# Four-layer block kernel on one core: pair products in four banks, decays between two gate products, and a reordered last-but-one block

## The reference

```python
# third layer, with h the state of 128 channels x 16
x_ssm, z = split(layernorm(x) @ W_in)
x_ssm = silu(causal_conv(x_ssm))          # 4 taps
dt = softplus(x_ssm @ dt_w + dt_b)
Bm, Cm = x_ssm @ B_w, x_ssm @ C_w
h = exp(min(dt * A, 0)) * h + (dt * x_ssm) * Bm      # step by step over time
y = h . Cm + x_ssm * D_param
out = residual + (y * silu(z)) @ W_out
# fourth layer, w1, w2, h1, h2, w3 ternary with a scale for each output
h = silu(x @ w1 * s1) * (x @ w2 * s2)
h = gelu(h @ h1 * t1)
h = gelu(h @ h2 * t2)
out = h @ w3 * s3
```

## Time and profile before

| | before |
|---|---|
| runs | 1028.96, 1021.58, 1022.63 us |
| median of the three | 1022.63 us |
| the profiled execution | 1027.38 us |
| its span in the trace | 1025.6 us |
| PE, DVE, ACT, POOL busy | 858.2, 681.8, 573.3, 446.5 us |
| mean granted clock of PE | 0.864 of full |

### The profile page before, as it was taken

One profiled execution on the slowest core, in us unless ns is written; L12 is line 12 of the kernel. 1 busy time (PEld: TensorE's weight loads), 2 busy tenths in 40 slices (PEclk: granted clock), 3 DMA queues, 4 the chain that ended last, 5 costly groups with the idle time before them and its releaser, 6 DMA issues.

```text
span 1025.6 us, 21514 instructions
## 1 busy us (share of the span) xinstructions
PE 858.2 (84%) x8256; PEld 694.7 (68%) x8256; DVE 681.8 (66%) x1997; ACT 573.3 (56%) x1072; POOL 446.5 (44%) x771
## 2 busy tenths in 40 slices
PE   4888845789999999897678669999798988887995
PEld 4777735668888888776546457778576766766774
DVE  4877864757888887652487768676876858673431
ACT  3444532346666666556467467565858667444541
POOL 1755762314555554434367544335353524341000
PEclk9766865559999999887687779999999999999898
DMA  8300002000000000000000000000000000000000
GB/s 274 100 13 17 24 22 64 22 1 2 2 2 2 2 3 2 1 2 1 1 0 1 1 0 2 1 0 12 1 11 1 12 1 6 6 11 0 11 1 20
DMA packets 22149, 16.76 MB, mean 16 GB/s; under 512 B 2576, under 2 KB 20376, under 8 KB 21792
## 3 DMA queue, kind: packets, MB, share of 16 engines
q1 hardware_dynamic: 21040, 14.77, 4.7%
q10 hardware_dynamic: 1008, 0.63, 0.2%
HBM read 11.20 MB, written 4.19 MB: 15 GB/s over the span
## 4 chain that ended last, share of the span: by engine, by line
PE 65%; DVE 17%; ACT 8%; issue 5%; POOL 3%; DMA 1%; ACTq 0%; POOLq 0%; SPq 0%; DVEq 0%
PE ps L1580 12%; PE ps L1582 9%; PE ps L1581 9%; PE ps L1659 6%; PE ps L1593 6%; PE ps L1881 3%; PE ps L1999 3%; PE ps L1652 2%; PE ps L1575 2%; PE ps L1599 2%; PE ps L1935 1%; DVE vbd L1047 1%; PE ps L1941 1%; PE ps L1683 1%; DVE a_ln_st L108 1%
## 5 line engine op out<-in xcount | busy, mean ns | idle before, releaser
L1580 PE MATMUL ps<-h_h,wh_h 128*128 128x512 f32 x256 | 106.4, 416 | 10.6 <-DVE h_l L1429 6.5
L1582 PE MATMUL ps<-h_l,wh_h 128*128 128x512 f32 x256 | 101.7, 397 | 0.0
L1581 PE MATMUL ps<-h_h,wh_l 128*128 128x512 f32 x256 | 101.5, 396 | 0.0
L1659 PE MATMUL ps<-w_e,he 128*128 128x128 f32 x512 | 87.0, 310 | 3.7 <-ACT he L719 3.3
L719 ACT ACTIVATE he<-ps,pp 128x256 f32<-128x256 f32 x128 | 59.6, 471 | 43.5 <-PE ps L1582 39.0
L1659 PEld LDWEIGHTS ps<-w_e,he 128*128 128x128 f32 x512 | 76.9, 221 | 6.1 <-ACT he L719 5.4
L1593 PEld LDWEIGHTS ps<-mov,hbd 32*128 32x128 f32 x2048 | 78.5, 233 | 0.0
L1593 PE MATMUL ps<-mov,hbd 32*128 32x32 f32 (+1 forms) x2048 | 77.4, 308 | 0.0
L577 POOL TENSOR_TENSOR term<-term 128x224 f32<-128x224 f32 (+2 forms) x48 | 38.9, 811 | 84.2 <-DVE term L1316 81.7
L1580 PEld LDWEIGHTS ps<-h_h,wh_h 128*128 128x128 f32 x256 | 49.2, 192 | 27.0 <-DVE h_l L1429 9.0
L117 POOL TENSOR_TENSOR b_ln_ve<-b_ln_mv,eps 128x2 f32<-128x2 f32 x64 | 13.1, 204 | 110.9 <-DVE b_ln_mv L111 110.9
(11 more groups left out here) (292 smaller groups left out, 2581.6 us busy)
## 6 DMA issues: line engine op xcount, KB each, us to landing
x<-in_x SPq DMA_DIRECT2D x16, 128.0 KB
w_h<-in_w_h SPq DMA_DIRECT2D x2, 1024.0 KB, 8.3
x<-x SPq DMA_DIRECT2D x16, 128.0 KB, 1.8
xB<-x SPq DMA_DIRECT2D x32, 64.0 KB
out_x<-xB SPq DMA_DIRECT2D x32, 64.0 KB
w_m<-in_w_m SPq DMA_DIRECT2D x3, 256.0 KB, 5.8
xB<-in_w_e SPq DMA_DIRECT2D x1, 512.0 KB
w_e<-in_w_e SPq DMA_DIRECT2D x1, 512.0 KB
```

What stands on the lines that cost most here:

```text
L1580: pe.matmul(dst, a_h, b_h, start=start, stop=True, skip_group_check=True)
L1581: pe.matmul(dst, a_l, b_h, start=False, stop=True, skip_group_check=True)
L1582: return pe.matmul(dst, a_h, b_l, start=False, stop=True, skip_group_check=True)
L1659: last = pe.matmul(ps[:, ACC, P * c:P * c + P], he[e % 2][:, P * c:P * c + P], w_e2[:, e, :], start=False, stop=True, skip_group_check=True)
```

## The change

1. Steps 0 to 3 (`WHOLE = 4`): `pairs` makes all four groups at once, into banks 4 to 7, at the place in the step before where it made two. `terms` multiplies all four in one pair of instructions of twice the size. On DVE, in these steps, `add_sums` goes ahead of `step_size`, the sums of dt and the statistics ahead of the weighted input, and `bbd` behind the states.
2. Every step with a block that enters: ACT makes the next tile's decays between the gates of parts 0 and 1, no longer behind part 1; the high part of part 0 goes into the next step, behind `parts_of_step`. ACT_TABLE_LOADs in the program: 109 before, 119 after.
3. Every step with a middle block: PE makes `inputs_by_chunk` ahead of `outputs_by_chunk`, no longer behind the convolution. In step 15, where there is no next tile, `gate_and_up` of part 3 goes behind `pairs`, `chunk_weights` and `chunk_states`, and ACT's `chunk_weights` ahead of the high part 2.
4. Step 16: PE makes all four `gate_and_up` of block 6 in a row and then `last_product` of block 5, which stood behind part 0. Other banks serve blocks 6 and 7, block 5's second hidden layer goes to `hid_behind`, and ACT's order at the tail's start follows. DVE's order of the tail is unchanged.

The diff, cut to its core:

```diff
@@ -368,8 +369,8 @@
                 return TAIL_HIDDEN[b - LAST + 1][w][m]
             return 6 + m % 2
-        TAIL_UP = {(LAST - 1, 2): 4, (LAST - 1, 3): 2, (LAST, 0): 2, (LAST, 1): 4, (LAST, 2): 2, (LAST, 3): 4}
-        TAIL_HIDDEN = (((6, 7, 0, 1), (6, 7, 0, 1)), ((7, 0, 1, 2), (3, 4, 5, 7)))
+        TAIL_UP = {(LAST - 1, 1): 4, (LAST - 1, 2): 0, (LAST, 0): 2, (LAST, 1): 6, (LAST, 2): 2, (LAST, 3): 6}
+        TAIL_HIDDEN = (((4, 5, 0, 1), (4, 5, 0, 1)), ((5, 0, 1, 2), (3, 6, 7, 5)))
         def turned_bank(b):
...
-            return {LAST - 1: 6, LAST: 0}.get(b, BR)
+            return {LAST - 1: 4, LAST: 0}.get(b, BR)
         def block_of(n, behind):
                 act.wait_ge(m_h2_ps, nth(b, m))
-                dst = hid_behind if b >= LAST - 1 else hid
+                dst = hid_behind if b >= LAST - 2 else hid
                 act.activation(dst[:, m, :], ps[:, hidden_bank(b, 1, m), :], ACT.Gelu, scale=vec("h2_s", m)).then_inc(m_h2, 1)
...
                     parts_of_step(n + 1)
+                if middle is not None:
+                    high0(middle, 0)
                 if have(2):
                     transposed_input(n + 2)
                 if have(1):
@@ -956,22 +959,23 @@
                 if have(2):
                     silus(n + 2)
                 if middle is not None:
+                    if not have(1) and have(0):
+                        chunk_weights(n)
                     high0(middle, 2)
                     gated(middle, 3)
-                    if have(0):
+                    if have(1):
                         chunk_weights(n)
                     high0(middle, 3)
                 if entering is not None:
                     gated(entering, 0)
+                if have(1):
+                    decays(n + 1)
+                if entering is not None:
                     if have(-2):
                         output_norm(n - 2)
                     if have(0):
                         states_out(n)
                     gated(entering, 1)
-                if have(1):
-                    decays(n + 1)
-                if entering is not None:
-                    high0(entering, 0)
                 if middle is not None:
                     hidden1(middle, 0)
                 if entering is None and have(-2):
                 b, c = LAST - 1, LAST
+                gated(b, 2)
+                high0(b, 0)
+                high0(b, 1)
+                gated(b, 3)
                 output_norm(NB - 1)
-                high0(b, 1)
-                gated(b, 2)
-                gated(b, 3)
                 high0(b, 2)
                 high0(b, 3)
                 hidden1(b, 0)
                         dve.wait_ge(S["c_bcT"], t + 2)
-                dve.wait_ge(S["c_g1_ps"], 2 * t + k + 1)
+                if t < WHOLE:
+                    if k == 1:
+                        return
+                    lo, hi, count = 0, 4, 2
+                    dve.wait_ge(S["c_g1_ps"], 2 * t + 2)
+                else:
+                    lo, hi, count = 2 * k, 2 * k + 2, 1
+                    dve.wait_ge(S["c_g1_ps"], 2 * t + k + 1)
                 w = wall[l][:, :, :, :].rearrange("p c s t -> p s c t")
-                split = lambda v: v.rearrange("p s (g c) t -> p s g c t", g=4)[:, :, 2 * k:2 * k + 2]
...
+                                  banks[:, :, 0:WIDE].rearrange("p g (s c t) -> p s g c t", s=HALF, t=CH), ALU.mult)
                 dve.tensor_tensor(split(term[l][:, HALF * PAIR:].rearrange("p (s c t) -> p s c t", s=HALF, t=HALF)),
                                   split(w[:, 0:HALF, :, HALF:CH]),
-                                  ps[:, PAIRS:PAIRS + 2, WIDE:BC_AT].rearrange("p g (s c t) -> p s g c t", s=HALF, t=HALF),
-                                  ALU.mult).then_inc(S["c_term"], 1)
+                                  banks[:, :, WIDE:BC_AT].rearrange("p g (s c t) -> p s g c t", s=HALF, t=HALF),
+                                  ALU.mult).then_inc(S["c_term"], count)
             def add_sums(t):
                 l = t % 2
@@ -1471,6 +1484,8 @@
                     raised(middle, 2)
                 if have(0):
                     terms(n, 0)
+                if n < WHOLE and have(-1):
+                    add_sums(n - 1)
                 if have(1):
                     step_size(n + 1)
                 if entering is not None:
                     low0(middle, 3)
-                elif have(1):
+                elif have(1) and n >= WHOLE:
                     summed_steps(n + 1)
                 if have(-1):
-                    add_sums(n - 1)
+                    if n >= WHOLE:
+                        add_sums(n - 1)
                     gated(n - 1)
+                if n < WHOLE:
+                    summed_steps(n + 1)
+                    statistics(n + 4)
                 if have(1):
                     weighted_input(n + 1)
                 if leaving is not None:
                     output_normed(leaving)
                 if have(0):
                     carried(n)
-                if have(1):
+                if n >= WHOLE and have(1):
                     inputs_by_chunk(n + 1)
                 if have(-1):
                     residual(n - 1)
                 if have(0):
                     states(n)
+                if n < WHOLE:
+                    inputs_by_chunk(n + 1)
                 if entering is not None:
                     tokens_low(entering)
-                if have(4):
+                if n >= WHOLE and have(4):
                     statistics(n + 4)
                 if entering is not None:
                     raised(entering, 0)
@@ -1922,6 +1943,8 @@
             def pairs(t, k):
                 l = t % 2
+                if t < WHOLE and k == 1:
+                    return
                 if k == 0:
                     pe.wait_ge(S["c_prod"], t + 1)
                 if t == 0 and k == 0:
                     pe.wait_ge(S["c_term"], 2 * t + k)
-                for g in range(2):
-                    part = heads(2 * k + g)
-                    last = pe.matmul(ps[:, PAIRS + g, 0:BC_AT], ones[part, :], prod[l][part, :], start=True, stop=True)
-                last.then_inc(S["c_g1_ps"], 1)
+                groups = range(4) if t < WHOLE else (2 * k, 2 * k + 1)
+                for i, g in enumerate(groups):
+                    last = pe.matmul(ps[:, PAIRS + i, 0:BC_AT], ones[heads(g), :], prod[l][heads(g), :], start=True, stop=True)
+                last.then_inc(S["c_g1_ps"], len(groups) // 2)
             def turned_states(t):
                 pe.wait_ge(S["c_hs"], t + 1)
                         pe.wait_ge(m_h2, nth(b - 1, HID - 1))
-                elif b < LAST - 1 or b == LAST - 1 and m == 1:
+                elif b < LAST - 1:
                     pe.wait_ge(m_raw, nth(b, m - 1))
+                elif b == LAST - 1 and m == 1:
+                    pe.wait_ge(S["c_term"], 2 * NB)
+                elif b == LAST - 1 and m == 3:
+                    pe.wait_ge(m_raw, nth(b, 0))
                 elif b == LAST and m >= 2:
                     pe.wait_ge(m_raw, nth(b, m - 2))
                 cols = slice(P * m, P * m + P)
@@ -2017,15 +2044,15 @@
                     from_states(n - 1)
                 if ending is not None:
                     hidden(ending, 1, 0)
+                if middle is not None and have(1):
+                    inputs_by_chunk(n + 1)
                 if have(1):
                     outputs_by_chunk(n + 1)
                 if middle is not None:
                     gate_and_up(middle, 2)
                 if have(2):
                     convolved(n + 2)
-                if middle is not None:
-                    if have(1):
-                        inputs_by_chunk(n + 1)
+                if middle is not None and have(1):
                     gate_and_up(middle, 3)
                 if have(0):
                     pairs(n, 1)
                     chunk_states(n)
+                if middle is not None and not have(1):
+                    gate_and_up(middle, 3)
                 if middle is not None:
                     if have(1):
                         pairs(n + 1, 0)
@@ -2060,21 +2089,22 @@
                     hidden(middle, 0, 3)
                 if entering is not None:
                     gate_and_up(entering, 0)
+                if n == NB:
+                    gate_and_up(entering, 1)
+                    pe.wait_ge(c_ln2.mv_ready, NB)
+                    gate_and_up(entering, 2)
+                    gate_and_up(entering, 3)
                 if ending is not None:
                     last_product(ending)
-                if entering is not None:
+                if entering is not None and n < NB:
                     gate_and_up(entering, 1)
             def tail():
                 b, c = LAST - 1, LAST
-                pe.wait_ge(c_ln2.mv_ready, NB)
-                pe.wait_ge(S["c_term"], 2 * NB)
-                pe.wait_ge(S["d_yr"], LAST - 1)
-                for m in range(2, HID):
```

(5 more changed lines are left out.)

3 lines of the change are left out of this document (2 added, 1 removed).

## The result

The changed kernel took 1039.12 us (median of four, 1034.04 to 1042.36) against 1022.15 us: a ratio of 1.0146, with a 95% interval of 1.0087 to 1.0206. The prediction was 1015.5 us, 1007.5 to 1022.5. Its profiled execution took 1038.8 us, of which the span is 1037.0, at a granted clock of 0.849 (before: 1027.38, 1025.6, 0.864). So it is slower by about 1.5%, and the traces differ by 11.4 us.

A forecast was written before the change was run, and what follows sets the result against it. DVE was taken to bound steps 0 to 3; with blocks, ACT early in the middle step, then DVE and PE in turn. Terms -11.5 + 0.5 + 1.8 + 2.1 = -7.1 us from the median 1022.63 gave 1015.5 us, range 1007.5 to 1022.5.

The forecast's parts named there:

- Where the bound lies, and that DVE would run through in steps 0 to 3: Steps 0 to 3: DVE leads and would be busy over 95%; waiting for chunk states would show the forecast wrong.
- Part 1, -11.5 us: Steps 0 to 3: 13.2 us gained from DVE's waits, less 1.7 for POOL's contention; range -14.3 to -7.5.
- Gates 1 and 2, the merged wait of 3.7 us, the loads without a drain: Block pairs: gate 1 0.5 us late, `raw` 0.35 earlier, one PE wait of 3.7 us, 1.30 us per load.
- Rival (d): ACT's table switches drain, 1.4 us more each, gate 2 some 3 us late per pair: +8, 1031 us; 3%.
- Parts 2 and 3, +0.5 us: Pairs of steps 5 to 14: low clock costs net +0.45 us in four, one gains 0.7; range -2.5 to +4.
- Rival (c): Block pairs: PE runs at 0.50 after its 3.7 us wait, up to 3 us lost each: +7, 1030 us; 7%.
- Step 15, +1.8 us, range to 3.5: Step 15: decays ready sooner gain 0.9 us, but part 3 behind pair sums and chunk states delays `raw` 3.
- Tail, +2.1 us: Step 16 and tail: `last_product` behind all four parts makes `scaled` 5.1 us late, `hidden(6, 0, 0)` +2.1 us (+1 to +3).
- The sum: Whole kernel: -11.5 + 0.5 + 1.8 + 2.1 = -7.1 us, taken from the median, 1015.5 us.

The follow-up runs named there:

- no_split: Kernel before with only the whole pair sums of steps 0 to 3, POOL's weight splits in steps 0 to 4 cut to 8 of 512 columns; ratio 0.9866.
- filled: Changed kernel plus 12 small fp32 products on PE in its wait before part 3's `gate_and_up`, steps 5 to 13; ratio 0.9965 against the kernel before.
- both_moves: Kernel before with only ACT's decays moved between gates of parts 0 and 1, and `inputs_by_chunk` ahead of `outputs_by_chunk`; ratio 1.0151.
- kept_filled2: Kernel before with changes 1, 2 and 3 without step 15's, plus small PE products in waits of steps 5 to 13, 15 and before `hidden(6, 0, 0)`; 0.9884.
- tail_only: Kernel before with change 4 alone (step 16 and the tail); ratio 1.0052.

## Why the prediction was wrong

- **Where the bound lies, and that DVE would run through in steps 0 to 3:** right in the main. DVE is busy for 94% of them, where I had said over 95%, and it waits 0.40 us for the chunk states in step 0, which I had named as a sign of being wrong; it is too short to matter.
- **Part 1, -11.5 us:** right in kind, 2.7 us short to the entry. Two terms were mis-sized. For POOL's contention I took 1.7 us from bounds of 0 and 5.6. The splits alone cost 5.8 in the new steps (no_split), and the decay products grew by 5.5 over before, since before the splits lay beside DVE's waits, terms and dt instead. But DVE's other instructions shrank by 3.5, of which I had counted 0.4, so the net is 2.4 where I had 1.7. The larger part, 2.0 us, is idle time: 3.5 us where my layout left 1.5 (1.09 at the entry for 0.3, the two short waits, and 1.8 between instructions for 0.8).
- **Gates 1 and 2, the merged wait of 3.7 us, the loads without a drain:** right to 0.1 us each (5.48 and 8.67; 3.80; the decay starts 1.29 us behind the load). Rival (d) is out: the Exp follows its load at 772.52, and filled gains in spite of the ten loads.
- **Parts 2 and 3, +0.5 us: here the prediction failed.** The mechanism was seen and its size was wrong. The step is the price of the low clock, "six matrix instructions cost 2.95 us there, not 1.7", about 0.85 us a pair. I saw that the clock would fall, and let the low level end with part 3. It lasted 10 to 14 us in eleven of twelve cases, over the pair sums, the chunk states and half of the first `hidden`, and cost 3.5 us a pair. The 6 us behind a shorter wait said that part 3 was no bound; I went by the 3 us of step 15. The sum of this term was off as well: four pairs at +0.45 and one at -0.7 make +1.1, not +0.5.
- **Rival (c)** was this mechanism, at 7% and 3 us a pair; it should have been the forecast. With 3.5 a pair and its other terms as they stand it gives +9.9 us; the traces show +14.1 apart from the untouched stages, and the rest is part 1 (+1.9 with the stretch behind the entry) and the end (+2.3).
- **Step 15, +1.8 us, range to 3.5:** measured +4.6. The gain of the decays is there (both_moves has the stretch 1.1 us shorter than before, 0.9 predicted), but the order costs 2.9 us and the clock 3.3 more, behind the wait for terms and the one ahead of `hidden(5, 0, 0)` (from kept_filled2's 47.12, which is 1.6 under before: -1.6 + 2.9 + 3.3). I had counted half clock for gate 3 only, not for the pair sums and chunk states ahead of it, nor ACT's high part 2 behind `chunk_weights` as a wait of DVE.
- **Tail, +2.1 us:** 2.6 measured, of which 1.0 seemed to come back in this trace; tail_only gives 3.1 by its trace.
- **The sum:** -7.1 predicted, about +14 in the traces without the untouched stages; 17 of the 21 us between them lie in the five pairs.

## What to carry to other kernels

Don't merge two short waits of TensorE into a long one to save a fraction of a microsecond elsewhere: look at the granted clock behind each wait, and price a fall by everything that runs until the clock is back, not by the first instruction. Where the wait can't go, a few throwaway products in it, or a second wait that divides it, were each worth some 15 to 18 us here. Moves that cost little or nothing alone can cross such a point together, so measure the combination. And where an engine's idle time is squeezed out, count again what its neighbour on the memory does in the time that was idle.
